# A gated feed-forward kernel with a mixture of low-rank experts in float16 and float32r on one core: two loads of W placed elsewhere in the DMA queue, batch 1's x split one unit later, and some maxima and sums in another order on VectorE

## The reference

```python
# cond: x [4, 512, 1024] in float32, one language id per sequence
base   = einsum('btd,od->bto', x, W)
logits = einsum('btd,ed->bte', x, Wr) + one_hot(language_ids) * 5.0
topw, topi = top_k(logits, 2);  weights = softmax(topw)
gates  = sum(one_hot(topi) * weights)              # 8 experts, 2 of them
h      = einsum('btd,erd->bter', x, A)             # rank 16
y      = base + 2.0 * einsum('bter,bte,eor->bto', h, gates, B)
# ffn: W_gate, W_up [3584, 1024], W_down [1024, 3584], in float16
g = einsum('bsh,mh->bsm', y, W_gate);  u = einsum('bsh,mh->bsm', y, W_up)
out = x + einsum('bsm,hm->bsh', silu(g) * u, W_down)
```

## Time and profile before

| | |
|---|---|
| median of 3 runs | 1331.88 us |
| lowest, highest | 1331.61, 1333.08 us |
| profiled execution, its own time | 1332.57 us |
| its span in the profile | 1330.8 us |
| TensorE busy | 1323.1 us (99%) |
| VectorE, ScalarE, GpSimd busy | 802.7, 398.7, 126.2 us |
| granted TensorE clock, whole span | 1.00 |

### The profile page before, as it was taken

The page is one execution under the profiler, slowest core; times in us unless marked ns, Lnnn a source line. Parts: engine busy times, 40 slices in busy tenths (PEclk is TensorE's granted clock), DMA queues, the critical chain, the costliest instruction groups (busy, mean ns, idle before and its releaser), DMA issues.

```text
span 1330.8 us, 21543 instructions
## 1 busy us (share of the span) xinstructions
PE 1323.1 (99%) x8396; PEld 846.7 (64%) x8396; DVE 802.7 (60%) x1472; ACT 398.7 (30%) x653; POOL 126.2 (9%) x151
## 2 busy tenths in 40 slices
PE   9999999999999999999999999999999999999999
PEld 7854444445667666677666666667766666666666
DVE  7799697778614577764652555556373255545612
ACT  4365755463101344331011223332110122222000
POOL 3200011141000111100000111110000011111000
PEclk9999999999999999999999999999999999999999
DMA  9267977335865778853794568553387466656564
GB/s 342 86 230 286 374 287 258 128 107 197 311 212 149 276 259 313 322 187 111 252 332 149 185 228 277 182 168 111 101 309 270 145 185 186 182 185 211 166 232 138
DMA packets 117525, 286.97 MB, mean 216 GB/s; under 512 B 14128, under 2 KB 16816, under 8 KB 116656
## 3 DMA queue, kind: packets, MB, share of 16 engines
q1 hardware_dynamic: 117136, 285.43, 62.7%
q10 hardware_dynamic: 288, 0.16, 0.0%
HBM read 241.24 MB, written 44.30 MB: 215 GB/s over the span
## 4 chain that ended last, share of the span: by engine, by line
PE 82%; DVE 10%; DMA 4%; issue 1%; SPq 1%; ACT 1%; POOL 0%; DVEq 0%; ACTq 0%
PE banks L950 22%; PE banks L914 19%; PE banks L971 14%; PE banks L978 13%; PE banks L730 4%; PE banks L782 2%; DVE wmax_part L1498 2%; PE banks L906 2%; PE banks L907 2%; DMA down_dram<-wd_sum 1%; PE banks L1007 1%; DVE wd_sum L1487 1%; DMA w_raw<-W 1%; DMA wd_half<-Wd 1%; DMA gu_ring<-Wu 1%
## 5 line engine op out<-in xcount | busy, mean ns | idle before, releaser
L950 PE MATMUL banks<-y_hi,gu_ring 128*128 128x512 f16 x1344 | 316.5, 379 | 0.0
L950 PEld LDWEIGHTS banks<-y_hi,gu_ring 128*128 128x128 f16 x1344 | 131.5, 98 | 124.0
L971 PE MATMUL banks<-h,piece 128*128 128x512 f16 x840 | 188.5, 379 | 0.0
L906 PE MATMUL banks<-y_hi,gu_ring 128*128 128x512 f16 x432 | 163.7, 379 | 1.1 <-DMA gu_ring<-Wu 1.1
L907 PE MATMUL banks<-y_lo,gu_ring 128*128 128x512 f16 x432 | 163.7, 379 | 0.0
L971 PEld LDWEIGHTS banks<-h,piece 128*128 128x128 f16 x840 | 82.2, 98 | 89.7
L1820 ACT ACTIVATE sg<-banks,sc 128x512 f32<-128x512 f32 x112 | 76.1, 686 | 210.6 <-DVE banks L1555 129.6
L2038 POOL TENSOR_TENSOR m<-m,m 128x256 f32<-128x256 f32 x84 | 61.0, 726 | 667.6 <-DVE m L1536 667.6
L1558 DVE TENSOR_TENSOR banks<-banks,m 128x256 f32<-128x256 f32 x84 | 36.3, 432 | 126.5 <-PE banks L950 126.3
L978 PE MATMUL banks<-h,piece 128*128 128x256 f16 x896 | 106.1, 273 | 0.0
L978 PEld LDWEIGHTS banks<-h,piece 128*128 128x128 f16 x896 | 87.7, 98 | 19.7
(11 more groups left out here) (219 smaller groups left out, 1898.3 us busy)
## 6 DMA issues: line engine op xcount, KB each, us to landing
piece<-down_dram SPq DMA_DIRECT2D x80, 448.0 KB, 5.4
mix_c<-mix_dram SPq DMA_DIRECT2D x84, 384.0 KB, 4.0
gu_ring<-Wg SPq DMA_DIRECT2D x112, 256.0 KB, 3.0
gu_ring<-Wu SPq DMA_DIRECT2D x112, 256.0 KB, 3.0
piece<-Wd SPq DMA_DIRECT2D x64, 448.0 KB, 5.4
mix_a<-mix_dram SPq DMA_DIRECT2D x84, 256.0 KB, 2.7
mix_dram<-mixed SPq DMA_DIRECT2D x28, 640.0 KB, 3.7
wb<-w_dram SPq DMA_DIRECT2D x64, 256.0 KB, 3.6
```

The source lines that it names most:

```text
L906: MM(bank, w[:, k, :], y_hi[:, k, :], start=(k == 0), stop=False)
L950: mm = MM(bank, w[:, k, :], y_hi[:, k, :], start=False, stop=(k == KC - 1), skip_group_check=True)
L971: mm = MM(bank, w[:, k, :], h[:, half * MH + k, 0, :], start=(start and k == 0), stop=False, skip_group_check=True)
```

## The change

It has four parts.

1. In batch 0 the load of W's chunk 3 waits until chunk 0 of base(0) is multiplied. What stands behind it in the queue waits with it, batch 1's x first of all.
2. In batch 1 the load of W's chunk 3 stands ahead of the store of the last unit's mixed sums, where it stood behind it. On VectorE these five sums are made before `largest_weight` and the first `h` parts, where they were made after them and after the last two products.
3. The high and low parts of batch 1's x are made at units 18 to 25 of batch 0, not 17 to 24.
4. The maxima of batch 1's x: the first is taken at chunk 6 of base(0), the second and the third at chunk 7; before, the first two were taken at chunk 7 and the third after the routing of batch 1.

```diff
--- before.py
+++ after.py
@@ -115,7 +115,7 @@
 
     FIRST_LATE = 4
 
-    SPLIT_X = {17 + k: k for k in range(KC)}
+    SPLIT_X = {18 + k: k for k in range(KC)}
     SPLIT_W = {9 + 2 * i: i for i in range(EARLY_W)}
     LOAD_X = [15 if b == 0 else 4 for b in range(NB)]
     LOAD_W = {6 + 2 * i: i for i in range(EARLY_W)}
@@ -340,14 +340,16 @@
         @block.sync
         def _(sp):
             def load_w(b, o):
-                if o >= W_SLOTS:
+                if b == 0 and o == EARLY_W:
+                    sp.wait_ge(s_main, 1)
+                elif o >= W_SLOTS:
                     sp.wait_ge(s_main, OC * b + o - W_SLOTS + 1)
                     if b == 0:
                         sp.wait_ge(s_wmx, o - W_SLOTS + 1)
                 elif b:
                     sp.wait_ge(s_main, OC * b)
                     sp.wait_ge(s_wmx, OC)
-                    if o >= EARLY_W:
+                    if o == EARLY_W:
 
                         sp.wait_ge(s_g, MC * b)
                         sp.wait_ge(s_u, MC * b)
@@ -597,6 +599,8 @@
                         load_gu(b, s + GU_SLOTS)
                     if b and s + 3 < MC:
                         load_mix_c(MC * b + s + 3)
+                    if b == 0 and s == MC - 1:
+                        load_w(1, EARLY_W)
                     if b == 0:
                         store_mixed(s)
                         for q, c in DOWN_SUMS.get(s, ()):
@@ -604,7 +608,7 @@
                             if c == 4 and q + 2 < PAIRS:
                                 load_wd(q + 2)
                 if b == 0:
-                    for o in range(EARLY_W, OC):
+                    for o in range(EARLY_W + 1, OC):
                         load_w(b + 1, o)
                 elif b + 1 < NB:
                     rest_of_wb(b + 1)
@@ -1331,8 +1335,8 @@
                     if b and o == OC - 1:
                         h_sums(b - 1)
                     if b == 0 and o == OC - 1:
-                        x1_max(0)
                         x1_max(1)
+                        x1_max(2)
                     if b == 0 or o < 4:
                         chunk_max(b, o)
                     if b and o == OC - 1:
@@ -1346,6 +1350,8 @@
                         w_max({0: 4, 3: 5, 4: 6, 5: 7}[o])
                     if b == 0 and o in (0, 1, 2, 3, 5, 6):
                         x_max(o if o < 4 else o - 1)
+                    if b == 0 and o == OC - 2:
+                        x1_max(0)
 
             def a_parts(s):
 
@@ -1503,6 +1509,7 @@
                 for s in range(MC):
                     if s == MC - 1:
 
+                        weight_sums(s)
                         largest_weight()
                         rescale(0)
                         late_split(0, FIRST_LATE)
@@ -1515,7 +1522,8 @@
                     if s == MC - 2:
                         unit_max(MC - 1)
                         own_weight()
-                    weight_sums(s)
+                    if s < MC - 1:
+                        weight_sums(s)
                     for q, c in DOWN_SUMS.get(s, ()):
                         down_weight_sum(q, c)
                     if s == SCALES_AT:
@@ -1671,7 +1679,6 @@
             base(0)
             settle(0)
             route(1)
-            x1_max(2)
             x1_max(3)
             x_max(6)
             x_max(7)
```

## The result

The median went from 1332.07 us (15 runs) to 1329.23 us (15 runs, 1328.56 to 1330.11), 2.8 us less. The ratio of the runs is 0.9976, with a 95% interval of 0.9968 to 0.9984, which is 2.1 to 4.3 us. One of the 15 runs of the kernel before took 3615.58 us, which the median passes over. The profiled execution of the changed kernel took 1330.11 us and has a span of 1328.3 us; it was the slowest of its 15.

What follows compares the result with a forecast made beforehand. TensorE was taken as the bound, busy 1323.1 of 1330.8 us, so only its waits could be won. Terms -1.43 and -0.66, the rest 0, sum to -2.1 us: a median of 1329.8 us, range 1328.1 to 1332.0.

Steps and rivals of the forecast that it cites:

- within 0.2%: Whole kernel: a time within 0.2% of the kernel before, given 67%.
- faster: Whole kernel: faster by over 0.2%, below 1329.2 us, given 26%.
- The ceiling: TensorE's three pauses that the change can touch, 0.66, 1.28 and 1.43 us, 3.4 together, are the most it can gain.
- Part 1: Batch 1, W's chunk 3 loaded ahead of the last store: TensorE's wait before that chunk goes, -1.43 us.
- Part 2: Batch 0, W's chunk 3 loaded after chunk 0: the `hg` multiply is freed and the wait before the transposes goes, -0.66 us.
- Part 3: Moved maxima of x: y's low parts come 1.17 us later, within 1.7 us of slack, 0.5 left; term 0.
- Part 4: x's split a unit later: unit 19's weights can't come earlier by this and the splits end in time; term 0.
- the last sentence of part 4: Unit 19's 1.28 us wait stays, since VectorE's chain and TensorE both come 0.66 us earlier.
- rival A: The start's gain is swallowed, only chunk 3 of batch 1 counts: -1.43 us, 1330.5 us; 16%.
- Rival D: Batch 0's delayed loads come too late, chunk 5's cast delaying chunk 0's copy: +2.9 us, 1334.8 us; 6%.

Runs made afterwards that it cites:

- x alone late: The kernel before with only batch 1's x (and what queues behind it) held back, W's chunk 3 of batch 0 staying early: 1330.64 us against 1332.04.
- the run of part 3: The kernel before with only the maxima of batch 1's x moved: 1332.3 us against 1331.9.
- part 2: The kernel before with only W's chunk 3 of batch 0, and x of batch 1 behind it, asked for after chunk 0: 1330.72 us against 1331.9.
- x behind unit 19: The changed kernel with batch 1's x asked for behind the weights of unit 19: 1328.87 us, ratio 0.9978 to the kernel before.
- chunk 5 first: The changed kernel with W's chunk 5 of batch 0 asked for ahead of xm (x of batch 2): 1329.05 us, ratio 0.9977 to the kernel before.
- parts 1 and 2: The kernel before with both W chunk 3 load moves and the moved sums, without moved maxima or later split: together 1328.85 us against 1332.15.
- part 1: The kernel before with only W's chunk 3 of batch 1 loaded ahead of the last store and the sums made earlier: 1330.67 us against 1331.9.
- its load only: The kernel before with W's chunk 3 of batch 1 loaded ahead of the last store, sums left in place: 1330.8 us against 1332.15.
- parts 3 and 4: The kernel before with only the moved maxima, 1332.3 us, and with only the later split of batch 1's x, 1332.12 us; kernel before 1331.9.

## Why the prediction was right, and where it was off

The measured 1329.23 lies in the range of 1328.1 to 1332.0 and 0.6 below the forecast of 1329.8. I gave 67% to "within 0.2%". The medians are 0.21% apart, just over that bound, in the 26% that I gave to "faster"; the interval of 0.9968 to 0.9984 lies on both sides of it, so the runs do not decide between the two.

**The ceiling** held, more exactly than I could know: what was left after the three pauses and the start was the same within 0.1 us in all thirteen profiles. In the medians 2.8 to 3.3 of its 3.4 us were gained, where I had forecast 2.1.

**Part 1** went step by step: load out at 266.35 (worked out: 267.1 less 0.66), taken by ScalarE at 273.50 behind the sixth `h` (273.8), GpSimd done at 279.2 (280.3 less 0.66), slack 2.9 us (2.8). The size was a little low: the pause that it removes is 1.43 in the one profile I had, and 1.39 to 1.68 in the five that still had it (mean 1.50). That the sums need not move agrees with the profile and the median of the run without them; its interval does not settle it.

**Part 2** was right in its mechanism and mis-sized. W's chunk 3 took 3.6 us to land (3.3 taken), GpSimd got chunk 4 at 31.20 (not before 29.8), the multiply took 0.69 us, and the run with x alone late shows that chunk 4's place behind x is the cause. The term was 0.66; the five profiles with the old order at this point show 0.66, 0.80, 0.97, 1.22 and 0.77, a mean of 0.88. My one profile had the smallest. What the run of part 3 adds is that the multiply is only one place where the chain can be caught.

**Part 3** cost its 1.1 us of slack and nothing else, as worked out (0.5 expected to be left, 0.6 found). **Part 4** changed nothing.

**The step that failed is the last sentence of part 4**, that the 1.28 us at unit 19 stay. They are no fixed wait. Of the thirteen profiles in the table ten have none at all, part 2 has 0.33, the change 1.01, and the kernel before 1.28, the largest. In these profiles the load goes out somewhere between 191.05 (x behind unit 19) and 194.52 (before), and TensorE waits in those where that is 193.42 or later. The premise was right: VectorE's chain moved with TensorE's (unit 0's maximum came 0.74 us earlier, as TensorE did). What it left out is what comes between unit 0 and unit 19. VectorE waits there until stores of the down sums have landed and their buffers are free, and this differs from one execution to the next. VectorE's waits from 88 to 196 us (in total, times, longest) in the two profiles of the changed kernel, and with chunk 5 first:

```profile
DVE wd_sum L1493 <- DMA down_dram<-wd_sum: 11.8, 3, 6.4
DVE wd_sum L1493 <- DMA down_dram<-wd_sum: 10.5, 2, 5.6
DVE wd_sum L1493 <- DMA down_dram<-wd_sum: 9.3, 2, 5.4
```

The load of unit 19's weights went out at 193.95, 191.66 and 191.10. Most of the difference is in these waits and the rest in the start of the execution. So rival A, which needed this wait to swallow the start's gain, had less for it than I thought: it needs an execution that has the wait. That the wait was there in both profiles at hand, before and after, was chance.

**Rival D** did not come, but it was real: one chunk more of delay and it came with both its waits, at 2.7 us above the kernel before for 5.1 us of delay, where the prediction had 2.9 for 6.2.

**What stays open.** Alone, parts 1 and 2 gain 1.2 us each; together 3.3 on the second chip, and the whole change 2.8 in its own comparison. The pauses in the profiles explain 2.4 of it (0.88 and 1.50). From the ledger, the median execution of the kernel before must have 3.2 us of pauses, 1.7 of them outside chunk 3. The four other profiles with the old order (part 1, its load only, parts 3 and 4) show 0.8 to 1.2 at `hg` and none at unit 19. But those four are of executions 0.7 to 1.4 us shorter than the median of their kernel, so they may well lack a pause that the others have. One comparison points to `hg`: the kernel with only x held back differs from the kernel before at the start alone, and its median leaves just 0.3 us for pauses outside chunk 3. But that is an estimate from medians, well inside their intervals. Whether the 1.7 us hold a wait at unit 19 or a longer one at `hg` is not shown, and I tried no run that separates them.

## What to carry to other kernels

When an engine is 99% busy, the list of its waits is the ceiling of any reordering: add them up before weighing a change, and take each again from start to start, since rows that overlap hide part of a pause. A wait that hangs on a long chain of DMAs is a chance, not a constant: here three of thirteen profiles had it. Its size in a single profile is one draw and no term of a sum. And before a load is delayed on purpose, count what stands behind it in its queue and in the queue of the engine that consumes it: here 8.5 us of delay (the load out at 20.32 instead of 11.86) gained 1.2, and 5.1 more cost 5.5 to 5.9.

## What the runs showed of the hardware that I had not expected

- A blocked VectorE instruction need not be a big one: a `den` of 128x4 took 2.37 us beside a GpSimd subtraction of 2.39 that had started 0.05 us before it, and 0.17 without one. The Trainium skill (SBUF — State Buffer, "Who interferes with whom") says that VectorE and GpSimd share a pair of SBUF ports, that a VectorE `tensor_scalar` in a 2-port mode takes it too, and that whoever issues first has it for its whole instruction while the other is blocked. The rows agree in both directions, GpSimd's 2.82 against 2.40 behind VectorE's multiply among them; which mode the `den` ran in no row shows.
- The weights of unit 19 took 2.5 to 3.1 us from issue to landing ahead of 2 MB in the queue, and 8.7 to 10.0 us (in all profiles with that order) behind them.
- From one execution to the next, the first matmul of base(0) starts anywhere from 13.9 to 14.6 us; the two profiles of the changed kernel, one and the same program, have 14.59 and 13.94. That is a quarter of what the change gained.
